# Self-attention scores as two f32r products, with the high and low part of the queries in the two halves of each 32-row tile

## The reference

```
q = (x @ Wq.T + bq).reshape(b, n, 16, 16)      # k and v likewise
score = einsum('bihd,bjhd->bhij', q, k)
attn = softmax(score / 16, axis=-1)
o = einsum('bhij,bjhd->bihd', attn, v).reshape(b, n, f)
return o @ Wo.T + bo
```

## Time and profile before

| | |
|---|---|
| median of three runs | 1810.35 us |
| the profiled execution | 1810.3 us |
| its span, first to last instruction | 1808.5 us |
| PE busy | 1781.7 us (99%) |
| DVE busy | 1062.4 us (59%) |
| ACT busy | 970.0 us (54%) |
| POOL busy | 429.9 us (24%) |
| granted TensorE clock | 1.0 (2.4 GHz) in all 40 slices |

### The profile page before, as it was taken

How to read it: one execution, slowest core, us unless ns; L and a number is a source line. 1 busy time by engine, 2 the same in 40 slices (tenths; PEclk the granted TensorE clock), 3 DMA queues, 4 the chain that set the end, 5 groups by cost and what they waited for, 6 DMA issues and landing times.

```text
span 1808.5 us, 40567 instructions
## 1 busy us (share of the span) xinstructions
PE 1781.7 (99%) x17278; PEld 1596.0 (88%) x17278; DVE 1062.4 (59%) x2213; ACT 970.0 (54%) x1713; POOL 429.9 (24%) x351
## 2 busy tenths in 40 slices
PE   8999999999999999999999999999999999999998
PEld 7778898988989888898988989898898988989997
DVE  4555565655666556566556656556566656655553
ACT  3345755455555555545455555545545465555553
POOL 2102222222223122222222213222222212212222
PEclk9999999999999999999999999999999999999999
DMA  5000000000000000000000000000000000000000
GB/s 159 10 1 10 2 15 2 10 7 6 11 2 15 2 10 8 1 15 2 10 7 7 10 1 15 2 10 7 1 16 1 10 7 7 10 2 7 1 7 7
DMA packets 20851, 19.65 MB, mean 11 GB/s; under 512 B 9921, under 2 KB 19777, under 8 KB 20289
## 3 DMA queue, kind: packets, MB, share of 16 engines
q1 hardware_dynamic: 20672, 17.06, 3.4%
HBM read 12.86 MB, written 4.19 MB: 9 GB/s over the span
## 4 chain that ended last, share of the span: by engine, by line
PE 91%; DVE 4%; POOL 3%; ACT 2%; issue 1%; DMA 0%; POOLq 0%; DVEq 0%; SPq 0%; ACTq 0%
PE ps L458 22%; PE ps L459 20%; PE ps L460 20%; PE ps L546 4%; PE ps L566 3%; POOL h_lo L1396 3%; PE ps L583 2%; PE ps L677 2%; PE ps L693 2%; PE ps L836 2%; PE ps L658 2%; PE ps L768 1%; PE ps L613 1%; PE ps L759 1%; PE ps L500 1%; DVE h_hi L1278 1%
## 5 line engine op out<-in xcount | busy, mean ns | idle before, releaser
L1396 POOL TENSOR_TENSOR h_lo<-h_f,h_hi 128x512 fp32r<-128x512 f32 x256 | 336.2, 1323 | 1125.8 <-DVE h_hi L1278 1125.8
L458 PE MATMUL ps<-w_hi,h_hi 128*128 128x256 f32 x1024 | 299.4, 292 | 6.4 <-POOL h_lo L1396 4.6
L458 PE MATMUL ps<-sl_hi,w_hi 128*128 128x256 f32 x1024 | 302.4, 295 | 1.9 <-DVE sl_lo L1060 1.5
L459 PE MATMUL ps<-w_hi,h_lo 128*128 128x256 f32 x1024 | 289.3, 283 | 0.0
L459 PE MATMUL ps<-sl_hi,w_lo 128*128 128x256 f32 x1024 | 289.2, 282 | 0.0
L460 PE MATMUL ps<-sl_lo,w_hi 128*128 128x256 f32 x1024 | 289.1, 282 | 0.0
L460 PE MATMUL ps<-w_lo,h_hi 128*128 128x256 f32 x1024 | 289.1, 282 | 0.0
L1006 ACT ACTIVATE h_f<-ps 128x512 f32<-128x512 f32 x256 | 149.4, 597 | 143.0 <-PE ps L460 142.4
L1278 DVE CAST h_hi<-h_f 128x512 fp32r<-128x512 f32 x256 | 156.7, 622 | 118.0 <-ACT h_f L1006 117.6
L458 PEld LDWEIGHTS ps<-w_hi,h_hi 128*128 128x128 f32 x1024 | 195.1, 191 | 21.5 <-POOL h_lo L1396 18.5
L458 PEld LDWEIGHTS ps<-sl_hi,w_hi 128*128 128x128 f32 x1024 | 195.0, 190 | 20.2 <-issue 10.5
(11 more groups left out here) (202 smaller groups left out, 4106.1 us busy)
## 6 DMA issues: line engine op xcount, KB each, us to landing
x<-in_x SPq DMA_DIRECT2D x16, 256.0 KB, 2.7
out<-acc SPq DMA_DIRECT2D x16, 256.0 KB, 2.2
g_w<-in_w SPq DMA_DIRECT2D x2, 1024.0 KB, 12.2
cx<-in_ctxT SPq DMA_DIRECT2D x16, 77.0 KB, 2.0
g_wqk<-in_wqk SPq DMA_DIRECT2D x1, 1024.0 KB, 6.6
g_se<-in_se SPq DMA_DIRECT2D x1, 1024.0 KB, 8.6
biases<-in_bias SPq DMA_DIRECT2D x1, 640.0 KB, 4.8
mk_i<-in_mask SPq DMA_DIRECT2D x16, 38.5 KB
```

The source lines that it names most:

```text
L458: te.matmul(o, lhs[0], rhs[0], start=first, stop=False)
L459: te.matmul(o, lhs[1], rhs[0], start=False, stop=False)
L1396: Q_.tensor_tensor(h_lo[:, part, :], h_f[:, part, :], h_hi[:, part, :].bitcast(f32), ALU.subtract)\
```

## The change

The scores are made from f32r operands in two products. The new tile `qs` holds one head in each 32 rows: in the first 16 rows the high part of its queries, in the other 16 the low part. `k_hi` and `k_lo` hold the high and the low part of that head's keys, each written twice, in both halves. So `qs` times `k_hi` gives the high and the low part of the queries against the high part of the keys, and `qs` times `k_lo` adds both against the low part.

- `scores` and `shifted`: in the place of each group of 4 float32 matmuls (8 instructions) stand two groups of 4 f32r matmuls (8 instructions), accumulated in the same bank. The `ones` group stays.
- ACT: `k_step` is new, two instructions of 128x256 that bring k with its bias from PSUM to the tile `k`. `q_step` stays. `qh_step` and `kh_step` are new, one copy of 128x1024 each, from float32 to f32r.
- DVE: `km` and its four instructions go. `kd_step` and `qd_step` (function `twice`) spread a tile over its 32-row tiles, one head in each, in both halves: two STREAM_SHUFFLE each, 512 elements per partition. `qs_step` is one SCALAR_TENSOR_TENSOR of 128x1024, which subtracts the high part in the second half of each tile.
- POOL: `kl`, one TENSOR_TENSOR of 128x1024, makes `k_lo`.
- Memory: `k` lies over `xh_a`, `q_hi` over `xa_hi` and `xa_lo`. Hence new waits: DVE's `xh` of the next sequence on `k_d`, ACT's `xt` on `q_sb`, ACT's `qh` on `v_ps`. DVE's `kv` waits for `pv2` of the sequence before.
- The quad of q, k, v is free when `q_ev`, `k_ev` and `v_sb` have come; the first `scores` step of a sequence waits for `q_sb` (`qs` written) and `k_lo`.
- The lists `ORDER`, `START`, `FINISH`, `MISC` and `MISC_START` are written anew. `START` has 194 `idle` products in all in the place of 183; between `c0.v` and `c0.scores.0` stand 14 in the place of 3.

```
-    x_bo=1, q_ps=1, q_sb=1, k_ps=1, km=1, v_ps=1, v_sb=1,
+    x_bo=1, q_ps=1, q_ev=1, q_d=1, q_h=1, q_sb=1, k_ps=1, k_ev=1, k_d=1, k_h=1, k_lo=1, v_ps=1, v_sb=1,
...
-        s0.idle.8 c0.xt.1 s0.idle.18 c0.k c0.q c0.v s0.idle.3 c0.scores.0 s0.idle.10 c0.mt.0 s0.idle.4 c0.shifted.0
+        s0.idle.8 c0.xt.1 s0.idle.18 c0.k c0.q c0.v s0.idle.14 c0.scores.0 s0.idle.10 c0.mt.0 s0.idle.4 c0.shifted.0
...
-        km = sb("km", [P, 2, C, S])
+        k = at("k", [P, C, S], f32, r_xha)
+        r_qs, r_kl = region(4 * KB), region(4 * KB)
+        q_d, qs = at("q_d", [P, Q, S], f32, r_qs), at("qs", [P, Q, S], f32r, r_qs)
+        k_d, k_lo = at("k_d", [P, Q, S], f32, r_kl), at("k_lo", [P, Q, S], f32r, r_kl)
+        k_hi = sb("k_hi", [P, Q, S], f32r)
+        q_hi = at("q_hi", [P, Q, S], f32r, r_xa)
...
                 if n == 0:
                     pe.wait_ge(s["q_sb"], nth("q_sb", a, 1))
-                    pe.wait_ge(s["km"], nth("km", a, 1))
+                    pe.wait_ge(s["k_lo"], nth("k_lo", a, 1))
                 for t in range(NT):
-                    for i in range(R):
-                        rows = slice(32 * i, 32 * i + 32)
-                        last = te.matmul(ps[:, 1 + i, t * S:(t + 1) * S], q[rows, c, t * P:(t + 1) * P],
-                                         km[rows, e, c, :], start=True, stop=True)
+                    for keys, first in ((k_hi, True), (k_lo, False)):
+                        for i in range(R):
+                            rows = slice(32 * i, 32 * i + 32)
+                            last = te.matmul(ps[:, 1 + i, t * S:(t + 1) * S], qs[rows, n, t * P:(t + 1) * P],
+                                             keys[rows, n, :], start=first, stop=not first)
...
                 for j in range(NT):
-                    for i in range(R):
-                        rows = slice(32 * i, 32 * i + 32)
-                        te.matmul(ps[:, 1 + i, j * S:(j + 1) * S], km[rows, e, c, j * P:(j + 1) * P], q[rows, c, :],
-                                  start=True, stop=False)
+                    for keys, first in ((k_hi, True), (k_lo, False)):
+                        for i in range(R):
+                            rows = slice(32 * i, 32 * i + 32)
+                            te.matmul(ps[:, 1 + i, j * S:(j + 1) * S], keys[rows, n, j * P:(j + 1) * P], qs[rows, n, :],
+                                      start=first, stop=False)
...
+            def qh_step(a):
+                act.wait_ge(s["q_d"], nth("q_d", a, 1))
+                act.wait_ge(s["v_ps"], nth("v_ps", a, 1))
+                copy(q_hi[:, :, :], q_d[:, :, :]).then_inc(s["q_h"], 1)
+
+            def kh_step(a):
+                act.wait_ge(s["k_d"], nth("k_d", a, 1))
+                copy(k_hi[:, :, :], k_d[:, :, :]).then_inc(s["k_h"], 1)
...
+            def twice(o, i):
+
+                for e in range(2):
+                    last = V.stream_shuffle(o[:, e::2, :], i[:, :, :], [HD * e + r % HD for r in range(2 * HD)])
+                return last
...
+            def qs_step(a):
+
+                dve.wait_ge(s["q_h"], nth("q_h", a, 1))
+                V.scalar_tensor_tensor(qs[:, :, :], q_hi[:, :, :].bitcast(f32), cols[:, NMASK:NMASK + 1], q_d[:, :, :],
+                                       ALU.mult, ALU.add).then_inc(s["q_sb"], 1)
...
+            def kl(a):
+                pool.wait_ge(s["k_h"], nth("k_h", a, 1))
+                Q_.tensor_tensor(k_lo[:, :, :], k_d[:, :, :], k_hi[:, :, :].bitcast(f32), ALU.subtract)\
+                    .then_inc(s["k_lo"], 1)
```

More of the change, by code:

```diff
@@ L48 @@
     pe="""
[L49 to L53, removed]
+        m.lt.0 l.outer.3.0 d.kv m.dispatch.0 l.outer.3.1 c.xt.1 m.slots.0 l.comb.3 c.k c.q d.xt.2 c.v m.hidden.0.0
@@ L87 @@
[L87 to L101, removed]
@@ new lines @@
+        s0.idle.2 d0.scores2.1 d0.pv2.0 s0.idle.3 d0.mt2.1 c1.v s1.idle.1 d0.shifted2.1 d0.tr2.0 s1.idle.4 d0.ob2.0
+        c1.scores.0 d0.pv2.1 s1.idle.3 d0.tr2.1 s1.idle.4 c1.mt.0 s1.idle.4 d0.ob2.1 c1.shifted.0 d0.oproj2 s1.idle.1
+        c1.scores.1 c1.pv.0 s1.idle.6 c1.mt.1 s1.idle.5 c1.shifted.1 s1.idle.4 d0.xt.3 s1.idle.6 d0.logits.0
+        d0.logits.1 d0.logits.2 d0.logits.3 s1.idle.3 m0.lt.0 c1.scores.2 c1.pv.1 s1.idle.6 c1.mt.2 s1.idle.1
+        m0.dispatch.0 c1.shifted.2 c1.tr.0 m0.slots.0 c1.scores.3 c1.pv.2 s1.idle.2 c1.ob.0 m0.hidden.0.0 c1.mt.3
@@ new lines @@
+        m0.hidden.0.1 c1.shifted.3 d1.kv m0.hidden.0.2 s1.idle.1 c1.pv.3 s1.idle.2 c1.tr.1 m0.hidden.0.3 c1.ob.1
+        m0.lt.1 s1.idle.1 c1.oproj m0.outer.0.0 m0.dispatch.1 m0.outer.0.1 m0.comb.0 c2.xt.1 m0.slots.1 c2.k c2.q
+        c2.v m0.hidden.1.0 d1.xt.2 m0.hidden.1.1 c2.scores.0 m0.hidden.1.2 m0.hidden.1.3 m0.lt.2 c2.mt.0 m0.combine.0
+        c2.shifted.0 d1.q2 m0.dispatch.2 d1.scores2.0 c2.pv.0 m0.comb.1 d1.mt2.0 m0.slots.2 d1.shifted2.0
+        m0.outer.1.0 d1.scores2.1 d1.pv2.0 m0.hidden.2.0 d1.mt2.1 m0.outer.1.1 d1.shifted2.1 d1.tr2.0 m0.hidden.2.1
@@ L103 @@
+        c2.scores.1 d1.pv2.1 m0.hidden.2.2 c2.mt.1 m0.hidden.2.3 d1.ob2.0 c2.shifted.1 d1.tr2.1 m0.combine.1 m0.lt.3
+        d1.ob2.1 c2.scores.2 d1.oproj2 m0.outer.2.0 m0.dispatch.3 m0.outer.2.1 c2.mt.2 m0.slots.3 m0.comb.2 c2.pv.1
+        c2.shifted.2 c2.tr.0 m0.hidden.3.0 c2.scores.3 c2.pv.2 m0.hidden.3.1 c2.mt.3 m0.hidden.3.2 d1.xt.3
+        c2.shifted.3 m0.combine.2 m0.hidden.3.3 c2.ob.0 d1.logits.0 c2.pv.3 d1.logits.1 c2.tr.1 d1.logits.2 c2.ob.1
+        d1.logits.3 c2.oproj
     """,
@@ L886, in xt @@
                 act.wait_ge(s[f"xt{n}_ps"], nth(f"xt{n}_ps", a, 1))
+                if n == 1 and later(a):
+                    act.wait_ge(s["q_sb"], nth("q_sb", a - 1, 1))
                 copy((xa_hi if n == 1 else xd_hi)[:, :, :], halves(0)).then_inc(s[f"xt{n}_hi"], 1)
@@ L1090, in xh_step @@
                 dve.wait_ge(s[f"ln{n}_pw"], nth(f"ln{n}_pw", a, 1))
+                if n == 1 and later(a):
+                    dve.wait_ge(s["k_d"], nth("k_d", a - 1, 1))
                 scale = pw_n[:, 0, :]
@@ L1175, in kv @@
                 dve.wait_ge(s["kv_ps"], nth("kv_ps", a, 1))
+                if later(a):
+                    dve.wait_ge(s["pv2"], nth("pv2", a - 1, C))
                 for c in range(C):
```

232 lines of the change are left out of this document (123 added, 109 removed).

## The result

The changed kernel takes 1814.47 us (median of 13 runs, 1811.46 to 1819.22), the kernel before in the same runs 1810.15 us (1809.42 to 1812.25). The ratio is 1.0026, with a 95% interval of 1.0018 to 1.0035. The forecast was 1763 us, faster by 2.6%. The profiled execution took 1811.46 us, with a span of 1809.7.

A forecast was written before the change was run, and what follows sets the result against it. PE, busy for 1781.7 of 1808.5 us, was taken as the bound: 1810.3 - 50.7 for cheaper groups + 2.5 for the first sequence = 1762.1, plus 1 for small waits, 1763 us; range 1756 to 1778, the forecast's own 1758 to 1770.

The forecast's parts named there:

- The price of a group and of a step: On PE, four groups per step fall from 0.216 to 0.117 us each; 128 steps by 0.396 save 50.7 us.
- The rule of the Trainium skill quoted in the prediction: On PE, LDWEIGHTS overlaps matmuls only when row_grp differs; as a rival, groups stay at 0.216, 1812.8 us, chance 0.04.
- ACT: nothing: On ACT, 2.94 us more per sequence, 47 us over 16, fits into idle time and costs nothing.
- The shuffles: On DVE, four at 0.64 us each per sequence fit the tight stage, 10.3 of 14 us, and cost nothing.
- POOL, and the added waits: nothing: On POOL, `k_lo` takes 2.39 us and is there 1.2 us before `scores`; other new waits also cost nothing.
- `edt` ... that step comes no later than before: On DVE, `qs` stands ahead but the last sequence's output end moves behind the experts' `edt`, so it is no later.
- The first rival: In each loop turn the attention's operands, `k_lo`, `qs` or `h_lo`, come late: 0.95 to 1.5 us, 1774 to 1781, chance 0.17.
- For a list written anew ... I add 1 us: Small waits from the new instruction lists, 4.6 us and less now, can't be read from the trace: 1 us added.
- The first sequence: At the start, without cover, scores can start at about 20.1 us, 2.2 later; 2.5 us taken.

The follow-up runs named there:

- e1: The changed kernel with GpSimd's `k_lo` subtraction cut to 64 of 1024 columns, all but leaving out the keys' low part: 1776.98 us, ratio 0.9813.
- e2: The changed kernel with `k_lo` subtracted on VectorE instead of GpSimd, in the order `k_lo`, `edt`, `qs`: 1782.92 us, ratio 0.9846.
- e4: The kernel before, with an unneeded 128x2048 GpSimd subtraction added behind the first chunk's fourth `h_lo` in each turn: 1863.31 us, ratio 1.027.
- e7: The changed kernel with VectorE taking `edt` ahead of `qs` in each turn, all else as it is: 1798.64 us, ratio 0.9937.
- e8: e2 with `w_lo` back at its old START place, `pv2` ahead of the first scores, and the second chunk's second `h_hi` ahead of `m.pr.0`: 1778.68 us.
- e9: e8 without the matmuls on `k_lo` for the first three of sixteen batches, which the first sequence works on: 1775.27 us.

## Why the prediction was wrong, step by step

- **The price of a group and of a step: right.** 0.67 and 0.91 us measured for 0.69 and 0.92. Successive f32r groups of four in the same row tiles follow each other every 0.12 us. The rule of the Trainium skill quoted in the prediction would, as priced there, have left them at 0.216, and the trace does not follow it.
- **"ACT: nothing": right.** PE waits 1.3 us in all for ACT's exponentials (1.4 before), and 0.2 us, once, for `h_f`.
- **The shuffles: near.** A record is 0.75 us long, and the next starts 0.64 after it, as taken; by the figure of the Trainium skill, "VectorE: DVE Perf Modes", it was an estimated 0.6. In the window of the earlier trace rows VectorE is busy for 11.81 us, where 10.3 were forecast, and PE for all 14.00. The shuffles stop nothing.
- **"POOL, and the added waits: nothing": this is the step that failed.** I asked whether `k_lo` would be in time for the scores, and priced it at 2.39 us from the line between two GpSimd rows; alone it takes 2.36. The slack was counted for its reader alone. What it does to VectorE meanwhile was in no term, and neither was what `qs` does to it. Held `edt`: 13 x 1.79 = 23.3 us, where the term was 0. e1 and e2 take it away, e4 makes it without the change.
- **"`edt` ... that step comes no later than before"** was the cover under which this lay. I had compared what stands ahead of `edt` in the queue: `qs`, 1.55 us, for the output steps that moved behind it. That was near enough: `edt` starts 1.19 us after the fourth `h_lo` ends, for 0.92 before. It is its duration that grew. e7 shows that the order is worth 0.24 us a turn, with the clock left aside, and the hold the rest.
- **The first rival had the mechanism's outline** (late operands in each turn, 1774 to 1781), with the wrong operand, no held instruction and no clock. Its price, up to 1.5 us a turn, was 2.48 in fact. The row that could have shown the hold, the casts of two durations above, was in the trace of the kernel before.
- **The clock was in no term.** 10.4 us in the loop. The forecast had no stalls of this length, so it had no reason to look.
- **"For a list written anew ... I add 1 us": too little.** PE's waits for `h_lo` went from 4.6 to 10.4 us in its list. The second chunk has a new one in each turn, from start to start 0.60 us, 7.8 us in all. Each of GpSimd's four `h_lo` stands there 1.65 us from the next, since the VectorE cast in between, 0.42 us alone, ends only with GpSimd's instruction (up to 1.14 us). In the list before, `m.pr.0` stood behind the third of these casts; the new list has it behind the first. e8 puts it behind the second and got back 0.28 of the 0.60.
- **The first sequence: 3.7 us for the 2.5, and the gain behind them did not come.** The first scores start at 21.62 us against 20.1 to 20.7, mostly since `qs`, beside `k_lo`, took 2.07 us for 1.28. Of the 9.5 us that I counted for the start's 24 steps the matmuls did give up their time, but 11 more fillers, 22 instructions (55.6 us of them for 50.8), and longer waits stand in it, 3.2 us for `xh_a` and the slow clock behind it. By e9 little over a third of TensorE's time comes through there, so by this estimate some 6 of the 9.5 us were not to be had in any case; how the rest divides was not taken apart.

The time after e8, 1778.7 us, shows how far off the forecast is once the hold of `edt` and the low clock behind it are gone: 15.7 us above 1763, of which some 10 are 0.8 us a turn of small waits and most of the rest is the start.

## What to carry to other kernels

Before moving work to an idle GpSimd, list what VectorE does between SBUF and SBUF in that stretch, and who waits for it: the price of a GpSimd instruction is not its own slack but the hold on that work. When work is taken from the bounding engine, price the next operand of every stage as well; here TensorE was 99% busy, and still little over half of a second cut came through. And a stall of nearly 2 us on TensorE can cost more behind it, in low clock, than it does itself (up to 2.9 us for 1.8 in a turn here); where two short ones stood in its place the clock fell in 1 turn of 13, not in 5.
